# Latent attention in 64 by 64 tiles of TensorE, heads paired otherwise, with a new order table

## What is computed

```python
q_hk = (hidden_q @ Wq.T).reshape(b, s, H, K)            # H = 16 heads
q_big = einsum('bshk,hkq->bshq', q_hk, w_kc_q)
kv_rope = kv_c * cos[None] + _rotate_half(kv_c) * sin[None]   # 64 keys of 64 per sequence
q_r = einsum('bshq,hqr->bhsr', q_big, W_qr)
k_r = einsum('bld,hdr->bhlr', kv_rope, W_kr)
scores = einsum('bhsr,bhlr->bhsl', q_r, k_r)
attn = softmax(scores)
ctx_c = einsum('bhsl,bld->bhsd', attn, kv_rope)
out = einsum('bhsd,hkd->bshk', ctx_c, w_kc_kv).reshape(b, s, H * K) @ Wo.T
```

## Time and profile before

| | |
|---|---|
| median of 3 runs | 2221.48 us (2216.84 to 2698.34) |
| profiled execution | 2224.57 us, its span 2222.8 us |
| PE busy | 2111.8 us (95%), 13664 matmul records |
| DVE, ACT, POOL busy | 1390.2, 995.0, 643.7 us |
| mean granted clock of TensorE | 0.983 |

### The profile page before, as it was taken

The page is one execution under the profiler, slowest core; times in us unless marked ns, Lnnn a source line. Parts: engine busy times, 40 slices in busy tenths (PEclk is TensorE's granted clock), DMA queues, the critical chain, the costliest instruction groups (busy, mean ns, idle before and its releaser), DMA issues.

```text
span 2222.8 us, 37399 instructions
## 1 busy us (share of the span) xinstructions
PE 2111.8 (95%) x13664; PEld 1610.6 (72%) x13664; DVE 1390.2 (63%) x3453; ACT 995.0 (45%) x1974; POOL 643.7 (29%) x988
## 2 busy tenths in 40 slices
PE   6999999999999989899987789999999999999998
PEld 5888888888888768688765566666666666666655
DVE  3667767767787344233335777777777777777731
ACT  1445545554455334233333344555445455455442
POOL 1333334333333650200012333323333332333200
PEclk9999999999999999999999989999999999999999
DMA  6300050000000234332211200000000000000000
GB/s 176 108 13 13 27 190 10 11 18 10 9 13 13 100 116 141 99 112 72 69 55 44 69 23 24 20 14 17 24 25 25 25 25 25 25 25 24 15 6 7
DMA packets 82337, 102.00 MB, mean 46 GB/s; under 512 B 17129, under 2 KB 68465, under 8 KB 81649
## 3 DMA queue, kind: packets, MB, share of 16 engines
q1 hardware_dynamic: 76016, 82.84, 11.7%
q0 software_dynamic: 6144, 16.79, 2.3%
HBM read 62.90 MB, written 36.70 MB: 45 GB/s over the span
## 4 chain that ended last, share of the span: by engine, by line
PE 87%; DVE 5%; ACT 3%; issue 2%; another core or an unknown queue 2%; POOL 1%; DMA 1%; SPq 0%; ACTq 0%; POOLq 0%; DVEq 0%
PE ps L1960 14%; PE ps L1372 9%; PE ps L1985 7%; PE ps L366 6%; PE ps L766 5%; PE ps L725 5%; PE ps L1966 4%; PE ps L1470 3%; PE ps L736 3%; PE ps L415 3%; PE ps L757 2%; PE ps L1363 2%; PE ps L1976 2%; PE ps L1694 1%
## 5 line engine op out<-in xcount | busy, mean ns | idle before, releaser
L1372 PE MATMUL ps<-BIG,arena 128*128 x912 | 223.3, 394 | 25.0 <-DVE arena L1405 8.9
L1372 PEld LDWEIGHTS ps<-BIG,arena 128*128 128x128 f32 x912 | 172.8, 196 | 56.7 <-issue 34.4
L1408 DVE COPY arena<-ps 128x512 f32<-128x512 f32 x114 | 78.3, 689 | 145.5 <-PE ps L1372 132.3
L1960 PE MATMUL ps<-EARLY,arena 128*128 128x352 f32 x512 | 166.6, 468 | 0.0
L1960 PE MATMUL ps<-EARLY,BIG 128*128 128x352 f32 x512 | 166.6, 468 | 0.0
L1599 POOL DMA_INDIRECT arena<-results_by_slot,posi x64 | 63.3, 989 | 341.0 <-DVE X L1287 202.5
L366 PE MATMUL ps<-arena,EARLY 128*128 128x256 f32 x640 | 151.5, 388 | 0.0
L1428 ACT ACTIVATE arena<-ps,BIG 128x128 f32<-128x128 f32 x304 | 85.9, 374 | 112.3 <-PE ps L1363 94.7
L366 PEld LDWEIGHTS ps<-arena,EARLY 128*128 128x128 f32 x640 | 120.7, 193 | 19.8 <-issue 3.6
L1960 PEld LDWEIGHTS ps<-EARLY,BIG 128*128 128x128 f32 x512 | 92.7, 190 | 56.2 <-issue 12.2
L1960 PEld LDWEIGHTS ps<-EARLY,arena 128*128 128x128 f32 x512 | 92.7, 190 | 55.8 <-issue 10.8
(11 more groups left out here) (405 smaller groups left out, 4928.9 us busy)
## 6 DMA issues: line engine op xcount, KB each, us to landing
arena<-rows_by_slot SPq DMA_DIRECT2D x38, 256.0 KB, 2.6
results_by_slot<-arena SPq DMA_DIRECT2D x38, 256.0 KB, 2.1
rows_by_slot<-zrow SPq DMA_DIRECT2D x3, 2304.0 KB, 15.4
BIG<-in_moe_w SPq DMA_DIRECT2D x3, 1792.0 KB, 9.6
X<-in_x SPq DMA_DIRECT2D x8, 512.0 KB, 4.3
rows_by_token<-BIG SPq DMA_DIRECT2D x16, 256.0 KB
arena<-rows_by_token SPq DMA_DIRECT2D x16, 256.0 KB
back<-rows_by_token SPq DMA_DIRECT2D x16, 256.0 KB
```

Source lines behind the costliest of these rows:

```text
L1372: m = e.matmul(ps[:, q * 256:q * 256 + 256], src[:, q, c * P:c * P + P], BIG[:, bass.ds(pe_reg[ex.A.j0 + 2 * n + q] + (w0 + c * 256), 256) ...
L1960: e.matmul(ps[:, 0:352], L.hT[:, q, ts], WG[:, q, gs], start=q == 0, stop=False, skip_group_check=True)
```

## The change

The 16 heads are stacked otherwise in Bw: `wkc` and `wo` are permuted on loading. The queries stay in pairs (head 2q + a in rows 64a of qT's place q). `scores(i)` makes both banks of a half at once: 32 matmuls of 64 rows (a), 64 weight columns (b2) and 64 moving columns, taken from the diagonal blocks of BDT; bank a holds the heads of row half a. `attend(i)` is 8 matmuls of 64 rows (a), 64 weight columns (of BD's diagonal block a), 256 moving columns, to row half c of bank a. DVE, ACT and POOL work on Pm by column halves (64a) of all eight places instead of four whole places. `turn(i, 0)` therefore waits for both products of POOL, and `shift(1, 0)` for both turns of the first half. Pieces are ordered anew, one piece of scores a half instead of two, and all numbers of START and TURNS are new. pe_s3 waits in addition for its bank. BD is still cleared and transposed whole.

Of the table only lines are shown that the text speaks of.

```diff
@@ -39,86 +39,86 @@
...
-START = {"s1": [-5.81, 40.96, 87.92, 134.15, 181.93, 229.94, 272.61, 321.19, 370.43, 418.13, 467.16, 511.62, 558.16,
-         524.43, 552.87, 613.97, 656.07, 691.18, 756.68, 796.37, 839.23, 875.35], "prod": [-45.14, -22.18, 6.71,
-         21.59], "first": [-526.66], "x": [-9.42, 159.04, 303.49, 370.71, 439.75, 522.22, 538.25, 790.78], "tables":
-         "s4": [1207.58, 1276.67, 1545.22, 1604.61, 1665.18, 1725.95, 1789.21, 1850.3, 1913.11, 1973.74, 2035.04,
-         2343, 2404.92, 2470.31], "ffn": [1160.2], "moe": [1.5]}
...
-    "prod": {"sp": (-107,),
-              "sp": (347.65,),
-              "dve": (-352.79, -260.67)},
...
+START = {"s1": [-6.6, 45.48, 91.29, 136.76, 183.43, 229.51, 274.68, 320.21, 368.29, 411.28, 458.93, 507.16, 552.33,
+         474.01, 510.68, 570.42, 603.66, 652.22, 695.09, 756.91, 787.79, 823.3, 876.88], "prod": [-75.76, -13.16,
+         13.96, 37.94], "first": [-332.58], "x": [-13.9, 154.24, 311.01, 319.8, 373.29, 437.24, 444.21, 661.87],
+         1288.95, 1294.24], "s4": [1187.71, 1259.41, 1512.52, 1570.61, 1632.93, 1693.95, 1754.75, 1817.03, 1878.76,
+         "s6": [1514.87, 1575.78, 1636.67, 1697.97, 1759.75, 1821.42, 1883.42, 1945.95, 2007.84, 2069.29, 2131.92,
+         2193.04, 2254.56, 2315.98, 2378.61, 2441.31], "ffn": [1136.59], "moe": [1.5]}
...
+    "prod": {"sp": (-82.76,),
+              "sp": (201.44,),
+              "dve": (-424.2, -218.66)},
...
@@ -673,9 +673,9 @@
             s2.append(L)
-        s2v = steps("s2v", 2, "stat aggr var nm kv mx00 sb00 mx01 sb01 sm00 rc00 sm01 rc01 mx10 sb10 sm10 rc10 x0 "
-                              "mx11 sb11 sm11 rc11 x1")
-        s2a = steps("s2a", 2, "h hT kT q0 q1 q2 q3 ex00 ex01 pt00 ex10 pt01 cx00 cx01 ex11 pt10 pt11 cx10 cx11")
+        s2v = steps("s2v", 2, "stat aggr var nm kv mx00 sb00 mx01 sb01 sm00 rc00 sm01 rc01 mx10 sb10 mx11 sb11 sm10 rc10 "
+                              "sm11 rc11 x0 x1")
+        s2a = steps("s2a", 2, "h hT kT q0 q1 q2 q3 ex00 ex01 pt00 pt01 ex10 ex11 cx00 cx01 pt10 pt11 cx10 cx11")
         s2g = steps("s2g", 2, "zb rs mr rope np00 np01 np10 np11")
@@ -726,21 +726,29 @@
-            def scores(i, g):
-                ps = bank.take("s2", k(f"sc{i}{g}"), s2v, n, f"sb{i}{g}")
-                e.wait_ge(*s2a.at(n, "q1" if g == 0 else "q3"))
-                if bank.used(k(f"sc{i}{g}")):
-                    e.wait_ge(*bank.empty(k(f"sc{i}{g}")))
-                for q in range(4):
+            def scores(i):
+                for a in range(2):
+                    bank.take("s2", k(f"sc{i}{a}"), s2v, n, f"sb{i}{a}")
+                if i == 0:
+                    e.wait_ge(*s2a.at(n, "q3"))
+                for a in range(2):
+                    if bank.used(k(f"sc{i}{a}")):
+                        e.wait_ge(*bank.empty(k(f"sc{i}{a}")))
+                m = [None, None]
+                for q in range(8):
                     for b2 in range(2):
-                        m = e.matmul(ps[64 * b2:64 * b2 + 64, q * P:q * P + P],
-                                     L.qT[:, 4 * g + q, i * P + 64 * b2:i * P + 64 * b2 + 64], L.BDT[:, 2 * i + b2, :],
-                                     start=True, stop=True, skip_group_check=True)
-                m.then_inc(*bank.made(k(f"sc{i}{g}")))
+                        for a in range(2):
+                            rows = slice(64 * a, 64 * a + 64)
+                            m[a] = e.matmul(bank.of(k(f"sc{i}{a}"))[64 * b2:64 * b2 + 64, q * 64:q * 64 + 64],
+                                            L.qT[rows, q, i * P + 64 * b2:i * P + 64 * b2 + 64], L.BDT[rows, 2 * i + b2, rows],
+                                            start=True, stop=True, skip_group_check=True)
+                for a in range(2):
+                    m[a].then_inc(*bank.made(k(f"sc{i}{a}")))
...
                 ps = bank.take("s2", k(f"t{i}{g}"), s2a, n, f"pt{i}{g}")
-                e.wait_ge(*s2g.at(n, f"np{i}{g}"))
+                if g == 0:
+                    e.wait_ge(*s2g.at(n, f"np{i}1"))
                 if bank.used(k(f"t{i}{g}")):
@@ -748,14 +756,22 @@
             def attend(i):
+                for a in range(2):
+                    bank.take("s2", k(f"pv{i}{a}"), s2a, n, f"cx{i}{a}")
+                e.wait_ge(*s2a.at(n, f"pt{i}1"))
+                for a in range(2):
+                    if bank.used(k(f"pv{i}{a}")):
+                        e.wait_ge(*bank.empty(k(f"pv{i}{a}")))
+                m = [None, None]
                 for b2 in range(2):
-                    ps = bank.take("s2", k(f"pv{i}{b2}"), s2a, n, f"cx{i}{b2}")
-                    if b2 == 0:
-                        e.wait_ge(*s2a.at(n, f"pt{i}1"))
-                    if bank.used(k(f"pv{i}{b2}")):
-                        e.wait_ge(*bank.empty(k(f"pv{i}{b2}")))
-                    e.matmul(ps[:, :], L.BD[:, 2 * i + b2, :], L.PT[:, :, 64 * b2:64 * b2 + 64], start=True, stop=True,
-                             skip_group_check=True).then_inc(*bank.made(k(f"pv{i}{b2}")))
+                    for c in range(2):
+                        for a in range(2):
+                            rows = slice(64 * a, 64 * a + 64)
+                            m[a] = e.matmul(bank.of(k(f"pv{i}{a}"))[64 * c:64 * c + 64, b2 * 256:b2 * 256 + 256],
+                                            L.BD[rows, 2 * i + b2, rows], L.PT[rows, 4 * c:4 * c + 4, 64 * b2:64 * b2 + 64],
+                                            start=True, stop=True, skip_group_check=True)
+                for a in range(2):
+                    m[a].then_inc(*bank.made(k(f"pv{i}{a}")))
@@ -768,21 +784,17 @@
             yield
-            scores(0, 0)
-            yield
-            scores(0, 1)
+            scores(0)
             yield
...
             yield
-            scores(1, 0)
-            yield
             turn(0, 1)
             yield
+            scores(1)
+            yield
             attend(0)
...
             project(0)
-            yield
-            scores(1, 1)
             yield
@@ -809,24 +821,23 @@
-            def shift(i, g):
-                src = bank.of(k(f"sc{i}{g}"))[:, :].rearrange("p (h l) -> p h l", h=8)
-                m8 = L.mx[i][:, 8 * g:8 * g + 8]
-                e.wait_ge(*bank.full(k(f"sc{i}{g}")))
-                e.tensor_reduce(m8, src, AX, ALU.max).then_inc(*s2v.sig(n, f"mx{i}{g}"))
-                if i == 1:
-                    e.wait_ge(*bank.full(k(f"t0{g}")))
-                e.wait_ge(*s2v.at(n, f"mx{i}{g}"))
-                e.tensor_tensor(L.Pm[:, 4 * g:4 * g + 4, :].rearrange("p h (e l) -> p (h e) l", e=2), src,
-                                m8.unsqueeze(2).broadcast_to([P, 8, 64]), ALU.subtract).then_inc(*s2v.sig(n, f"sb{i}{g}"))
-
-            def total(i, g):
-                s8 = L.sums[i][:, 8 * g:8 * g + 8]
-                e.wait_ge(*s2a.at(n, f"ex{i}{g}"))
-                e.tensor_reduce(s8, L.Pm[:, 4 * g:4 * g + 4, :].rearrange("p h (e l) -> p (h e) l", e=2), AX,
-                                ALU.add).then_inc(*s2v.sig(n, f"sm{i}{g}"))
-                e.wait_ge(*s2v.at(n, f"sm{i}{g}"))
-                e.reciprocal(s8, s8).then_inc(*s2v.sig(n, f"rc{i}{g}"))
+            def shift(i, a):
+                src = bank.of(k(f"sc{i}{a}"))[:, :].rearrange("p (h l) -> p h l", h=8)
+                m8 = L.mx[i][:, 8 * a:8 * a + 8]
+                e.wait_ge(*bank.full(k(f"sc{i}{a}")))
+                e.tensor_reduce(m8, src, AX, ALU.max).then_inc(*s2v.sig(n, f"mx{i}{a}"))
+                if i == 1 and a == 0:
+                    e.wait_ge(*bank.full(k("t01")))
+                e.wait_ge(*s2v.at(n, f"mx{i}{a}"))
+                e.tensor_tensor(L.Pm[:, :, 64 * a:64 * a + 64], src, m8.unsqueeze(2).broadcast_to([P, 8, 64]),
+                                ALU.subtract).then_inc(*s2v.sig(n, f"sb{i}{a}"))
+
+            def total(i, a):
+                s8 = L.sums[i][:, 8 * a:8 * a + 8]
+                e.wait_ge(*s2a.at(n, f"ex{i}{a}"))
+                e.tensor_reduce(s8, L.Pm[:, :, 64 * a:64 * a + 64], AX, ALU.add).then_inc(*s2v.sig(n, f"sm{i}{a}"))
+                e.wait_ge(*s2v.at(n, f"sm{i}{a}"))
+                e.reciprocal(s8, s8).then_inc(*s2v.sig(n, f"rc{i}{a}"))
@@ -844,13 +855,13 @@
             yield
+            shift(1, 1)
+            yield
             total(1, 0)
             yield
+            total(1, 1)
+            yield
             add(0)
-            yield
-            shift(1, 1)
-            yield
-            total(1, 1)
             yield
@@ -887,10 +898,10 @@
-            def expo(i, g):
-                p = L.Pm[:, 4 * g:4 * g + 4, :].rearrange("p h (e l) -> p (h e) l", e=2)
-                e.wait_ge(*s2v.at(n, f"sb{i}{g}"))
-                e.activation(p, p, ACT.Exp).then_inc(*s2a.sig(n, f"ex{i}{g}"))
+            def expo(i, a):
+                p = L.Pm[:, :, 64 * a:64 * a + 64]
+                e.wait_ge(*s2v.at(n, f"sb{i}{a}"))
+                e.activation(p, p, ACT.Exp).then_inc(*s2a.sig(n, f"ex{i}{a}"))
```

(24 more changed lines are left out.)

## The result

| | before | changed |
|---|---|---|
| median | 2220.97 us | 2147.78 us (2144.75 to 2150.13, 4 runs) |
| ratio | 1 | 0.968 (95% interval 0.9663 to 0.9696) |
| profiled execution | 2224.57 us | 2144.75 us |

One of the four executions of the kernel before took 2698 us, and the ratio leaves it out.

A forecast was written before the change was run, and what follows sets the result against it. TensorE was taken to set the pace of blocks 2 to 13. Gains of 41 (attention), 6 (start) and 4 us (table), 51 in all, off 2224.57 gave 2173.6; forecast 2173 us, range 2148 to 2212.

The forecast's parts named there:

- the give-back: s1 to s3 loop: part of the saved PE work lost to other engines; of 52.8 us, 41 us arrive.
- Scores and contexts: Latent attention on PE: scores save 2.06 us a block, contexts 1.24; over 16 blocks 52.8 us less PE work.
- the bounds from single matmuls: Scores call on PE: 16 rounds bounded by moving columns and weight loads, 0.86 to 1.28 us.
- The slope of weight columns: Scores tiles on PE: 96 weight columns cost 94 ns, 128 cost 108, so 64 cost 80 ns.
- Case C: Attention tiles on PE: only two run at once; 2205 to 2232 us, most likely 2215; chance 0.06.
- 78% arrive: s1 to s3 loop: of 52.8 us PE work saved, 41 us reach the end time; ends 53 and 5.
- case E: All PE savings arrive and the table brings its high end; 2130 to 2150 us; sign idle under 6; chance 0.07.
- The moved waits: Softmax in s1 to s3: shift(1,0) waits for t01, turn(0,0) for np01; about 1.5 us in series twice a block.
- case B: Loop: four tiles at once but softmax chain bounds; 26 us instead of 41; 2190 to 2212 us; chance 0.28.
- The start: Kernel start: prod 0's loads go ahead of first, so prod 1's data arrive 6 us earlier (0 to 8).
- The rest of the table: Later stages, chiefly between starts of s4's second and third block: new numbers bring 4 us (-6 to +14).
- Case D: Loop: shift(1,0) holds DVE for t01 so long that PE stalls; 2266 us and above; chance 0.07.

The follow-up runs named there:

- the second comparison: Kernel before and changed kernel both run again unedited on chip 8: ratio 0.9728 (0.9692 to 0.9763), 60 us.
- e7: Changed kernel, scores call going through its four places one after another, eight matmuls at each: 2196.73 us, one execution.
- e5: Changed kernel, scores matmuls reordered: all of row half 0 first, then row half 1, neighbours differing in column place alone: 2149.08 us, one execution.
- e6: Changed kernel, scores matmuls reordered: all of column place 0 first, then column place 1, neighbours differing in row half alone: 2146.83 us, one execution.
- e4: Kernel before with shift(1,0) waiting for the second turn t01 instead of t00: 2224.24 us against 2216.06, ratio 1.0026.
- e12: Changed kernel with half of the projection left out (four of project's eight matmuls): 2096.95 us, ratio 0.9562.
- e1: Kernel before with only the contexts as 64 by 64 tiles (new attend, attended and stacking), old order table: 2217.02 us, ratio 0.9998.
- e11: Kernel before with half of the projection left out (four of project's eight matmuls), old order table: 2146.17 us, ratio 0.9773.
- e9: Changed kernel run again unedited on chip 8: 2132.19 us, ratio 0.9728.
- e10: Kernel before run again unedited on chip 8, for its trace: 2189.91 us, ratio 0.999 to its own runs.
- e3: Changed kernel with the old START and TURNS numbers for all stages from the tables on: 2194.78 us, ratio 0.9894.
- e2: Changed kernel with contexts taken back (attend, attended and stacking as before), new table kept: 2167.86 us, ratio 0.978.
- e8: Changed kernel with second DVE and POOL pieces of first put behind DVE's copy of prod 0's first product: 2130.04 us, ratio 0.9712.

## Why the forecast came out as it did

The direction and the cost of the tiles (within 0.03 us a call) were right. The size was 25 us short, and the median fell 0.2 us out of the range; in the second comparison the ratio would give 2161 us, inside it. The step that failed is the give-back: of the work taken from PE, 12 us were said not to arrive, and all of it arrived.

**Scores and contexts: right.** 1.13 us was taken for a scores call, 1.10 measured; 1.00 for a context call, 1.03 measured. The sum of 52.8 us of PE work was 58.7 by the groups' busy times, whose modelled ends overlap their neighbours, and about 55 from start to start (49.4 in the loop, an estimate for 16 blocks by the same rate). The neighbouring form with as many records (L1680, L1705) carried the estimate; the bounds from single matmuls (0.86 to 1.28) held it. The slope of weight columns gave 80 ns a record for one place, the plain ratio 54, the moving columns 56: e7 shows 58.

**The skill's rule.** The rule of the Trainium skill ("TensorE: Matmul & The Clock Gate", Part 3, The mechanism), by which a weight load runs beside matmuls of another row group only, would have made two at once the limit. Setting it aside on L736's 1.03 us was right: e5 has 1.84 us for two column places in one row half, e6 1.83 for two row halves. Case C is excluded. Whether it is the weight loads or the matmuls of the two that run side by side, the traces do not show, since the ends of both are modelled.

**"78% arrive": the step that failed.** The loop lost 53 us where PE lost 52 (653.9 to 601.8, 654.9 to 602.7). I gave back 12 us for a tenth of the chain off PE and for the softmax chain, and nothing of that came: PE's idle time did not grow. By the prediction's own sign, under 6 us of idle PE from 120 to 660 us is case E, and it is 2.2 us:

```profile
120.00:660.00 540.00, 537.79 (x4867) 471.73 (x4866) 406.98 (x1293) 293.47 (x511) 215.17 (x376) 1.00 0.11 35
```

The two premises were off as well. DVE did not rise to 79% of the loop but to 76 (458.6 of 606), being busy 25 us less there; and "0.5 us a block" for its waits on the scores misreads: 25.8 us over 13 blocks is 2.0 a block, 0.5 a call. The moved waits cost something under the old order (e4, 2 to 10 us) and lead PE's waits once PE is lighter (e12). In the changed kernel they cost PE 1.2 us in the loop (L755 on L962). That the new table is what covers them is argued: the changed kernel can't run under the old table, where the queues wait in a circle, but under the new one PE is idle only 1.5 of 669 us of the loop even with the scores in turn (e7). e1 shows that the give-back was not foolish: contexts alone, under the old order, lose three tenths in the loop and all by the end. It is not the rule for the old order either, since e11 passes on 43 of 47 us there. What decides the share that arrives stays open. Half of the gain lost, case B, did not happen; e12 shows waits of this kind at 42 us less PE work.

**The start: 6 us forecast, 7 and 5 found, the clock's part in it.** L609 started at 11.90 us instead of 18.73, near the 11 forecast. The copy did not run near 15 but at 21.34: I overlooked that DVE's second piece of `first`, whose number (-551) is also ahead of it, waits for the last constant loads. Prod 1's product starts at 29.88 instead of 31.15 us (29.42 against 32.23 in e9 and e10), and the first block of s1 is out 7 or 5 us earlier; the clock's rise has a share in that (at 51 us before and 44 changed in the first pair, 38 and 36 in the second). Before any of these moments the gain is the 1.3 and 2.8 us of prod 1's product.

**The rest of the table: 4 us forecast, about 9 to 11 found.** 4 to 6 between s2 and the experts, 5 behind the experts, in both comparisons. Not in the stretch I named alone; e3, with the old numbers there, loses both (18 us and 965 us in its trace). e3 mixes two tables, but e1, e4 and e11, which do not, have the old lengths too, and e2, e5, e6, e7, e8 and e12 the new ones, whatever their PE work: the late numbers bring it. What they do to the experts is open.

**What the forecast could not hold.** In the first comparison 8 us more are the end of s2 and the experts, where the kernel before happened to be slow; e9 and e10 have it with the other sign. So 53 + 7 + 6 + 5 = 71 of the 80 us have a place in the forecast's terms, and 53 + 5 + 4 + 5 = 67 less 8 in the second. Case E (2130 to 2150) came true by its time and by its first reason, all of the work arrived; that the first comparison reached 2148 is luck in part, since those 8 us are in it and the start and the table brought less than its 8 and 14. Case D shows no sign: the longest waits in the changed loop are 1.6 us for PE in all (L782 on L832).

## What to carry to other kernels

Take the cost of a packed matmul from a group with the same number of records and places, start to start, and check that neighbours in the order go to different places: the same 32 matmuls cost 1.10, 1.84 or 3.34 us by their order alone. When PE is busy 99% of a loop, expect most of the work taken from it to arrive: all of it here, where the order came anew with the change, 0.7 to 0.9 where it did not (e1, e11, e12). Parts of two orders mixed cost over half of the gain (e3). The new order with nearly the work of before left the time within 1% of before (e7, one execution); about 13 us of the gain are its own by that estimate. Compare stretches between fixed points of the work, in one session and on one chip, before an effect behind the changed part is believed, and see what work has moved across such a point (here half a block of the projection, 3.5 us).

## What the runs showed that I had not expected

The moment at which the clock of TensorE goes up at the start differs between executions of one kernel: 51 us in the first trace of before, 38 us in e10, although PE had worked without a long pause from 19 or 20 us on in both. Before it, L366 took up to 444 ns a record (8 in 3.55 us), the 1.2 GHz level; behind it 216, the 2.4 GHz level. This is read from the records' spacing: the profile's own granted clock has 1.00 for that first stretch. In e10 the clock fell once more, from 42 to 45 us, at a granted 0.53, with PE busy throughout. With the early rise the first block of s1 was out 4 us sooner (its last product began at 69.0 against 73.3 us). And the same kernel differs by 1.4% between sessions (medians 2190 and 2196 us on chip 8, 2191 on chip 15, 2216 on chip 0, 2221 in the first comparison); chip and session can't be told apart here. Between the traces of the first comparison and of e10 nearly all of it lies outside the dense loop, whose length agrees within 1 us (659 and 660).
